# 128-row products in an attention prologue and tail, padded key buffers, and another order of maxima, masks, units and PV

## The chip, the cores and the metric

The kernel runs on one core of one Trainium2 chip. The metric is the device time in microseconds of one execution. Five engines work side by side, each through its own list of instructions, and wait for each other by semaphores: TensorE (PE, its weight loads are PEld), VectorE (DVE), ScalarE (ACT), GpSimd (POOL) and SyncE (SP, which issues most transfers).

## The reference

A macaron layer over 2 x 1024 tokens of width 128: half a feed-forward network, attention, half a feed-forward network again, each with a layer norm in front and a residual around it.

```python
    x = L0_attn_hidden_states
    x = x + 0.5 * _L0_ffn_ref(_layernorm(x, axis=-1), ...)
    x = x + _L0_attn_ref(_layernorm(x, axis=-1), ...)
    x = x + 0.5 * _L0_ffn_ref(_layernorm(x, axis=-1), ...)
```

The network `_L0_ffn_ref` is a mixture of experts: one shared expert of 352 hidden channels and the best 2 of 7 routed ones. The attention has 16 heads of 8 channels and works causally; its keys are the normalised tokens themselves:

```python
        v = x @ w_v + v_b
        q = (x @ w_q + q_b) @ w_k.T + k_b
        kh = x.reshape(b, s, H, D).transpose(0, 2, 1, 3)
        scores = jnp.einsum('bhqd,bhkd->bhqk', qh, kh) * scale
        scores = jnp.where(causal[None, None], scores, mask_value)
        probs = jax.nn.softmax(scores, axis=-1)
        out = jnp.einsum('bhqk,bhkd->bhqd', probs, v)
        out = out @ c_proj_w + c_proj_b
```

## The kernel before

Three stages follow one another: the first network (`ffn_*` with f = 0), the attention (`attn_*`), the second network (f = 1).

The attention takes the 2 batches x 16 heads as 8 groups of four heads. Queries and keys of a group stand in SBUF as 128 rows: head j of the four has the rows 32j to 32j + 31 (`head_rows(j)`), in which high and low parts of its 8 channels stand, and two rows for the maximum. There are three buffers of each, `K.keys[v]` and `K.queries[v]`, used in turn. A score product takes only its head's 32 rows, so it fills a quarter of the rows of TensorE's array. Rows of the profile name it `32*128`.

A group is worked on twice. First come the **maxima**: 40 products of queries by keys (`m_unit_pe`, L1609), ten kinds (`MAX_ORDER`) by four heads, each into one bank of PSUM. DVE reduces each to its maximum (`ring_dve`, L1785). Sixteen of the 40 are unmasked and 512 keys wide. The other 24 touch the diagonal: ahead of the product, `mask_pe` (L1599) writes the mask into the bank with four small products of 32 columns, one per column group. Four banks (`RING`) are used in turn, so PE is at most four maxima ahead of DVE. After the last maximum DVE negates and splits them (L1789 to L1793), PE transposes them (`mrow`), and SP moves them into two rows of each head's queries (`rows_load`).

Then come the **units**: 40 products of keys by queries with the maximum already in them (`unit_pe`, L1652), in three banks in turn. ACT takes the exponential of each (L1841). GpSimd zeroes what lies above the diagonal (`mask_pool`, L1890), and twelve **PV** steps (`pv_pe`, L1693) multiply probabilities by values, four heads in the four column groups at once, on all 128 rows. Results go through ACT (`ot`), a transpose on PE (`out`) and a division on DVE.

The order of this work is written by hand. The prologue (`attn_pe`) runs the 40 maxima of group 0 and the first `LEAD` maxima of group 1; between them stand steps for the second batch (`SECOND_PE`, `SECOND_DVE`): layer norm (z, its transposes L590), the q products (L1498 to L1500) and the v products. From `UNITS_FROM` on, a unit of group 0 stands ahead of each maximum. Then eight bodies follow, one per group (`pe_body`): six of the kind LOOP, one LAST_BUT_ONE and one LAST. In a body run the rest of the next group's maxima, the first `LEAD` of the one after, the units from number 12 on and the next group's first 12, and the PV steps. `ORDERS` says with a letter each in which order PE takes them: K a mask, R the next of the ring (maximum, mrow or out), U a unit, a a PV step, E a step of what comes after the attention. `OUT_AT` and `MT_LATER` place the out and mrow steps among the maxima, and `OEV_BEHIND` ACT's copies of the output among its exponentials. LAST_BUT_ONE has maxima only in its first part, LAST has none; I call what follows the last maximum the tail.

SP loads keys and queries of the group after the next in each body (`stack_load`, `keys_load`). GpSimd scatters the rows of the networks (`scatter_pool`, L1214, and L1191), each followed in part of the list by a small memset as a pause (`pause_pool`, L1201).

Of the kernel before, what the change touches and what calls it, by code (L numbers as in the profile page):

```python
# [29 lines left out]
P = 128  # L30
# [116 lines left out]
MAX_ORDER = (1, 2, 0, 3, 6, 7, 8, 4, 5, 9)  # L147
# [64 lines left out]
LEAD = 22  # L212
MT_LATER = 3
OUT_AT = (10, 24)
# [23 lines left out]
ORDERS = ['KKRUURKaKKURRUURaKKKURRURUaaKKRURURKKRURUaKKUURRKKURURKKUURRRURaRUUURRRRURRUaRURRUUaURRUaUURRaRURURUKaKURRUKKRRUUKKaURRU', 'KKRUURKaKKURRUURaKKKURRURUaaKKRURURKKRURUaKKUURRKKURURKKUURRUaUUURRRUUaUEUUaUEUaUUaUUEUaUUUEUaUU', 'RUUaUUEUaUUEUEaaUUUUEaUUUUUUUEaUUURUUaUUUaUaaEaaW']  # L238
# [49 lines left out]
def place_memory(K, ctx):  # L288
# [65 lines left out]
    with ExitStack() as s:  # L354
        zt = [sb(f"zt_{part}", [P, TOKENS], F32R, scope=s) for part in ("h", "l")]
        with ExitStack() as s2:
# [106 lines left out]
    K.ranked = sem("ranked")  # L463
# [948 lines left out]
def pad_pool(K, f):  # L1412
# [3 lines left out]
    K.nc.gpsimd.memset(K.act[:, :, HID:], 0.0).then_inc(K.padded0, 1)  # L1416

# [186 lines left out]
def m_unit_pe(K, n, r_bank, u):  # L1604
# [11 lines left out]
def ring_pe(K, what, d, n, p, u, r, r_bank):  # L1616

    e, v = K.nc.tensor, (u + d) % 3
    if r >= len(RING) and not (what == "max" and masked(n)):
        e.wait_ge(K.A["taken"], r + 1 - len(RING))  # L1620
# [4 lines left out]
    if what == "max":  # L1625
        if n == 0:
            e.wait_ge(K.ld_k[v], 32 * loads(p, u, d))
        ins = m_unit_pe(K, n, r_bank, v)
# [11 lines left out]
def unit_pe(K, p, u, d, n, start=False):  # L1640
# [3 lines left out]
    v, at0 = (u + d) % 3, 0  # L1644
# [54 lines left out]
def pe_body(K, p, u, kind):  # L1699
# [4 lines left out]
    for what in ORDERS[kind]:  # L1704
        if what == "U":
# [687 lines left out]
```

## Time and profile before

| | |
|---|---|
| median of 3 runs | 572.92 us (568.94 to 573.08) |
| the profiled execution | 574.49 us, span 572.7 us |
| PE busy | 527.5 us, 92% of the span |
| PE weight loads | 374.0 us, 65% |
| DVE busy | 386.9 us, 68% |
| ACT busy | 320.7 us, 56% |
| POOL busy | 269.8 us, 47% |

The span is cut into 40 slices of 14.3 us here. A digit is the busy share in tenths; PEclk is the clock that TensorE was granted, in tenths of the full 2.4 GHz, so a 5 is 1.2 GHz:

```profile
PE   5988879989999999999999999999899989899995
DVE  4696635557396397989999999973453775445744
ACT  4553434448343247787777878777555434434643
PEclk9899989999955558999999999979758999899998
```

The attention lies between about 157 and 437 us, slices 11 to 30. The groups that cost most of it, with the mean of one in ns and the idle time of the engine ahead of them:

```profile
L1785 DVE TENSOR_REDUCE mxp<-psum 128x1 f32<-128x512 f32 (+3 forms) x320 | 181.0, 630 | 32.3 <-PE psum L1609 32.2
L1841 ACT ACTIVATE probs<-psum 128x512 f32<-128x512 f32 x256 | 136.7, 600 | 45.1 <-PE psum L1652 44.1
L1609 PE MATMUL psum<-keys,queries 32*128 32x512 f32 (+3 forms) x384 | 107.7, 465 | 1.2 <-DVE mxp L1785 1.0
```

### The profile page before, as it was taken

What the parts mean: (1) busy time and instruction counts of PE and PEld (TensorE: products, weight loads), DVE (VectorE), ACT (ScalarE), POOL (GpSimd) and SP (SyncE); (2) the same over time, 40 slices, a digit from 0 to 9 for tenths busy, and PEclk for the clock granted to TensorE, in tenths of its full rate; (3) what the DMA queues carried; (4) which work ended last, traced back from release to release, by engine and by line L of the source; (5) the groups of instructions that cost most, each with busy time, mean ns of one, the idle gap of its engine ahead of it and who ended that gap; (6) DMA issues with size and microseconds to landing.
All of it is one profiled execution on the core that took longest, in us unless ns stands there. A gap on an engine that the chain in (4) does not pass through costs nothing.

```text
span 572.7 us, 12932 instructions
## 1 busy us (share of the span) xinstructions
PE 527.5 (92%) x4358; PEld 374.0 (65%) x4358; DVE 386.9 (68%) x1029; ACT 320.7 (56%) x694; POOL 269.8 (47%) x417
## 2 busy tenths in 40 slices
PE   5988879989999999999999999999899989899995
PEld 2888879988845654453444444345445889899994
DVE  4696635557396397989999999973453775445744
ACT  4553434448343247787777878777555434434643
POOL 8299887656583310304131111111308888854440
PEclk9899989999955558999999999979758999899998
DMA  8921424132761250405142231200001031431414
GB/s 280 291 70 48 113 75 126 43 103 85 229 181 46 74 186 2 175 2 174 28 149 79 99 137 39 102 2 2 2 0 34 30 90 43 123 90 41 130 39 116
DMA packets 40814, 52.65 MB, mean 92 GB/s; under 512 B 5616, under 2 KB 31728, under 8 KB 40112
## 3 DMA queue, kind: packets, MB, share of 16 engines
q1 hardware_dynamic: 31088, 39.03, 22.5%
q0 software_dynamic: 4480, 9.25, 4.9%
q10 hardware_dynamic: 5184, 3.55, 2.1%
q8 instruction: 38, 0.62, 0.5%
q14 instruction: 24, 0.20, 0.1%
HBM read 31.93 MB, written 28.00 MB: 105 GB/s over the span
## 4 chain that ended last, share of the span: by engine, by line
PE 51%; DVE 25%; issue 12%; DMA 5%; SPq 4%; POOL 2%; ACT 1%; DVEq 0%; ACTq 0%; POOLq 0%
DVE mxp L1785 19%; PE psum L1609 8%; PE psum L950 7%; PE psum L1693 6%; PE psum L1652 5%; PE psum L936 4%; PE psum L918 4%; PE psum L1599 3%; PE psum L916 3%; PE psum L917 3%; SPq L1275 2%; DMA wall_f<-in_ffn_sd 1%; DMA yc<-y_rows 1%; PE psum L1636 1%; POOL z_rows L1191 1%
## 5 line engine op out<-in xcount | busy, mean ns | idle before, releaser
L1785 DVE TENSOR_REDUCE mxp<-psum 128x1 f32<-128x512 f32 (+3 forms) x320 | 181.0, 630 | 32.3 <-PE psum L1609 32.2
L1841 ACT ACTIVATE probs<-psum 128x512 f32<-128x512 f32 x256 | 136.7, 600 | 45.1 <-PE psum L1652 44.1
L1609 PE MATMUL psum<-keys,queries 32*128 32x512 f32 (+3 forms) x384 | 107.7, 465 | 1.2 <-DVE mxp L1785 1.0
L1017 ACT ACTIVATE silu<-psum 128x352 f32<-128x352 f32 x107 | 49.6, 463 | 95.5 <-PE psum L918 70.2
L1652 PE MATMUL psum<-queries,keys 32*128 32x512 f32 (+3 forms) x384 | 99.7, 446 | 1.8 <-ACT probs L1841 1.8
L1214 POOL DMA_INDIRECT y_rows<-ys,to_row x76 | 74.2, 977 | 56.7 <-DVE ys L1096 30.7
L1060 DVE TENSOR_TENSOR act<-silu,psum 128x352 f32<-128x352 f32 x107 | 55.5, 519 | 65.1 <-ACT silu L1017 35.1
L950 PE MATMUL psum<-wall_f,at 128*128 (+1 forms) x648 | 92.1, 279 | 2.4 <-DVE x L1098 1.7
L1890 POOL TENSOR_SCALAR_AFFINE_SELECT probs<-probs 128x512 f32<-128x512 f32 x48 | 29.5, 635 | 131.6 <-ACT probs L1841 131.6
L950 PEld LDWEIGHTS psum<-wall_f,at 128*128 128x128 f32 x648 | 82.0, 194 | 3.8 <-issue 2.6
L1693 PE MATMUL psum<-probs,vg 128*32 128x512 f32 (+2 forms) x640 | 76.8, 555 | 0.0
L1652 PEld LDWEIGHTS psum<-queries,keys 32*128 32x128 f32 x384 | 50.6, 196 | 40.1 <-ACT probs L1841 18.7
L1609 PEld LDWEIGHTS psum<-keys,queries 32*128 32x128 f32 x384 | 50.4, 203 | 32.7 <-DVE mxp L1785 24.8
L936 PE MATMUL psum<-ident,act 128*128 128x128 f32 x324 | 54.6, 278 | 7.5 <-DVE act L1060 6.7
L916 PE MATMUL psum<-wall,zs_h 128*128 x152 | 56.5, 372 | 1.7 <-DVE zs_l L1084 1.7
L1025 ACT COPY at<-psum 128x384 f32<-128x384 f32 x108 | 51.3, 475 | 11.4 <-PE psum L936 8.1
L1599 PEld LDWEIGHTS psum<-ident_b,mask_b 128*32 128x32 bf16 x768 | 20.6, 97 | 47.1 <-DVE mxp L1785 27.8
L1599 PE MATMUL psum<-ident_b,mask_b 128*32 128x128 bf16 (+1 forms) x768 | 46.0, 261 | 5.1 <-DVE mxp L1785 3.6
L917 PE MATMUL psum<-wall,zs_h 128*128 x152 | 50.2, 330 | 0.0
L918 PE MATMUL psum<-wall,zs_l 128*128 x152 | 50.0, 329 | 0.0
L936 PEld LDWEIGHTS psum<-ident,act 128*128 128x128 f32 x324 | 41.0, 142 | 13.4 <-DVE act L1060 10.2
L1191 POOL DMA_INDIRECT z_rows<-zrow,slots x32 | 34.8, 1086 | 16.1 <-DVE slots L767 10.8
(245 smaller groups left out, 798.3 us busy)
## 6 DMA issues: line engine op xcount, KB each, us to landing
z_rows<-q_stack SPq DMA_DIRECT2D x12, 682.5 KB, 5.8
keys<-k_stack SPq DMA_DIRECT2D x8, 512.0 KB, 6.3
queries<-q_stack SPq DMA_DIRECT2D x8, 512.0 KB, 5.1
zg_early<-z_rows SPq DMA_DIRECT2D x44, 65.0 KB
yc<-y_rows SPq DMA_DIRECT2D x10, 256.0 KB, 4.2
zg_late<-z_rows SPq DMA_DIRECT2D x32, 65.0 KB
yc<-y_rows ACTq DMA_DIRECT2D x6, 256.0 KB, 4.1
wall_f<-in_ffn_rd SPq DMA_DIRECT2D x1, 1344.0 KB, 16.8
```

What stands on the lines that cost most here:

```text
L916: e.matmul(dst, zh, weight(K.wall, base, hi, HID), start=True, stop=False)
L917: e.matmul(dst, zh, weight(K.wall, base, lo, HID), start=False, stop=False)
L918: ins = e.matmul(dst, zl, weight(K.wall, base, hi, HID), start=False, stop=True)
L936: ins = e.transpose(bank(K, at_bank(f, q))[:, k * P:(k + 1) * P], K.act[:, q % 2, k * P:(k + 1) * P], K.ident[:, :])
L950: ins = e.matmul(bank(K, Y_BANK)[:, 0:EMB], K.at[:, q % 2, k * P:(k + 1) * P], weight(K.wall_f, base, DN + k * EMB, EMB), start=(k == 0), ...
L1214: e.indirect_dma_start(K.y_dram[f], bass.IndirectOffsetOnAxis(ap=K.to_row[:, j:j + 1], axis=0), K.ys[:, j % RING_Y, :], None).then_inc(K.y ...
L1599: e.matmul(dst[:, :, (nb - 1) * P:], K.mask_b[:, head_rows(c)], K.ident_b[:, :].unsqueeze(1).to_broadcast([P, len(parts), P]), start=True, ...
L1609: ins = K.nc.tensor.matmul(bank(K, r_bank)[:, start:start + nb * P], K.queries[u][head_rows(j), i * P:(i + 1) * P], K.keys[u][head_rows(j) ...
L1652: ins = e.matmul(slot(K, u, d, n)[:, at0:at0 + q1 - q0], K.keys[v][head_rows(j), kt * P:(kt + 1) * P], K.queries[v][head_rows(j), q0:q1], ...
L1693: ins = e.matmul(bank(K, O_BANK)[32 * j:32 * j + 32, q0 - half * CHUNK:q1 - half * CHUNK], K.vg[:, kt, j, :], probs_of(K, n)[:, j, :], sta ...
L1785: e.tensor_reduce(dst, scores, AX.X, ALU.max).then_inc(K.A["taken"], 1)
L1841: e.activation(strip_of(K, w)[:, j, :], slot(K, u, d, n)[:, 0:strip_width(w)], ACT.Exp, scale=SCALE).then_inc(K.A["ex"], 1)
```

## The change

It has four parts.

1. The key buffers become four times as large: `K.keys[v]` is [128, 4, 1024], and head j's keys stand in its 32 rows of slice j. `keys_load` loads them with four transfers in place of one. For the buffers 0 and 1 GpSimd fills the whole with zeros before (`wipe_pool`, 16 memsets, in place of the pauses behind the scatters 10 to 25 of the first network), and SP waits for these before the first load of keys. `probs_narrow` moves to another place in SBUF.
2. With them a product can take all 128 rows: the other heads' rows meet zeros. `m_whole_pe` does so for a maximum, with one mask product of 128 columns behind the product instead of four of 32 ahead of it; `unit_pe` with `whole` does so for a unit. All maxima and units of the prologue are of this kind, and the units behind the last maximum: the letters u in the orders of LAST_BUT_ONE and LAST. The loop's products stay at 32 rows.
3. `LEAD` is 20, not 22: the prologue has 62 steps of the ring and not 64, and LAST_BUT_ONE two maxima more.
4. `MAX_ORDER`, `OUT_AT`, `MT_LATER`, `OEV_BEHIND` and the three `ORDERS` are others.

```diff
-MAX_ORDER = (1, 2, 0, 3, 6, 7, 8, 4, 5, 9)
+MAX_ORDER = (0, 1, 3, 2, 6, 7, 4, 8, 5, 9)
-LEAD = 22
-MT_LATER = 3
-OUT_AT = (10, 24)
+LEAD = 20
+MT_LATER = 2
+OUT_AT = (0, 24)
...
-        if j < (WHOLE if f else WHOLE + 16):
+        if j < WHOLE:
             pause_pool(K)
+        elif f == 0 and j < WHOLE + 2 * WIPES:
+            wipe_pool(K, *divmod(j - WHOLE, WIPES))
...
+def wipe_pool(K, u, part):
+
+    e, n = K.nc.gpsimd, SEQ // 2
+    if (u, part) == (0, 0):
+        e.wait_ge(K.w_lo, len(WEIGHTS))
+        e.wait_ge(K.sw_lo, 5)
+        e.wait_ge(K.ld["const"], 16 * N_CONST_DMA)
+    j, half = divmod(part, 2)
+    e.memset(K.keys[u][:, j, half * n:(half + 1) * n].bitcast(F32), 0.0).then_inc(K.wiped, 1)
...
-                                 K.keys[u][head_rows(j), k0 * P:(k0 + nb) * P], start=not masked(n), stop=True,
+                                 K.keys[u][head_rows(j), j, k0 * P:(k0 + nb) * P], start=not masked(n), stop=True,
...
+def m_whole_pe(K, n, r_bank, u):
+
+
+    e, (parts, j) = K.nc.tensor, MAXES[n]
+    nb = parts[0][2]
+    dst = bank(K, r_bank)[:, 0:len(parts) * nb * P].rearrange("p (a k) -> p a k", k=nb * P)
+    for a, (i, k0, _) in enumerate(parts):
+        ins = e.matmul(dst[:, a, :], K.queries[u][:, i * P:(i + 1) * P], K.keys[u][:, j, k0 * P:(k0 + nb) * P],
+                       start=True, stop=True, skip_group_check=True)
+    if masked(n):
+        ins = e.matmul(dst[:, :, (nb - 1) * P:], K.mask_b[:, :],
+                       K.ident_b[:, :].unsqueeze(1).to_broadcast([P, len(parts), P]), start=False, stop=True,
+                       skip_group_check=True)
+    return ins
...
-    v, at0 = (u + d) % 3, 0
+    v, at0, rows = (u + d) % 3, 0, slice(0, P) if whole else head_rows(j)
...
-        ins = e.matmul(slot(K, u, d, n)[:, at0:at0 + q1 - q0], K.keys[v][head_rows(j), kt * P:(kt + 1) * P],
-                       K.queries[v][head_rows(j), q0:q1], start=True, stop=True, skip_group_check=True)
+        ins = e.matmul(slot(K, u, d, n)[:, at0:at0 + q1 - q0], K.keys[v][rows, j, kt * P:(kt + 1) * P],
+                       K.queries[v][rows, q0:q1], start=True, stop=True, skip_group_check=True)
...
-    K.nc.sync.dma_start(K.keys[v][:, :].bitcast(F32), K.k_dram[at(row, 4)].rearrange("g r t -> (g r) t"))\
-     .then_inc(K.ld_k[v], 16)
+    for j in range(4):
+        K.nc.sync.dma_start(K.keys[v][32 * j:32 * j + 32, j, :].bitcast(F32),
+                            K.k_dram[at(row + j, 1)].rearrange("g r t -> (g r) t")).then_inc(K.ld_k[v], 16)
...
-    e.wait_ge(K.w_lo, len(WEIGHTS))
-    e.wait_ge(K.sw_lo, 5)
+    e.wait_ge(K.wiped, 2 * WIPES)
     keys_load(K, 0, 0, 0)
```

What this makes of TensorE's list shows at three places. A row is a line, the operation, its output, its two operands and its size, and xN says that N like it follow one another. Lines are those of each kernel: products of maxima are L1609 before and L1637 (128 rows) or L1623 (32 rows) now, masks L1599 and L1640 or L1613, units L1652 and L1682, PV L1693 and L1723, out transposes L1636 and L1666.

TensorE in the prologue, from the first group's sixteen unmasked maxima on. Before:

```order
L1609 MATMUL psum<-keys,queries 128x512 x16
L1599 MATMUL psum<-ident_b,mask_b 32x128 x4
L1609 MATMUL psum<-keys,queries 128x384
L1599 MATMUL psum<-ident_b,mask_b 32x128 x4
L1609 MATMUL psum<-keys,queries 128x384
```

Now:

```order
L1637 MATMUL psum<-keys,queries 128x512 x16
L1637 MATMUL psum<-keys,queries 128x384
L1640 MATMUL psum<-ident_b,mask_b 128x128
L1637 MATMUL psum<-keys,queries 128x384
L1640 MATMUL psum<-ident_b,mask_b 128x128
```

The four small masks ahead of a product have become one behind it.

TensorE where the first loop body meets its first PV of 512 columns. Before:

```order
L1609 MATMUL psum<-keys,queries 128x384
L1652 MATMUL psum<-queries,keys 128x512 x2
L1609 MATMUL psum<-keys,queries 128x384
L1599 MATMUL psum<-ident_b,mask_b 32x2x128 x4
L1693 MATMUL psum<-probs,vg 32x512 x4
L1599 MATMUL psum<-ident_b,mask_b 32x2x128 x8
```

Now:

```order
L1682 MATMUL psum<-queries,keys 128x512 x2
L1666 MATMUL psum<-ident,ot 128x128 x4
L1613 MATMUL psum<-ident_b,mask_b 32x128 x12
L1623 MATMUL psum<-keys,queries 128x384 x3
L1723 MATMUL psum<-probs,vg 32x512 x4
L1613 MATMUL psum<-ident_b,mask_b 32x128 x8
L1682 MATMUL psum<-queries,keys 128x512
L1623 MATMUL psum<-keys,queries 128x384
```

The out transposes have come to the head of the body, and three masks and three products in one piece ahead of the PV.

TensorE in the last body, at the step that feeds the slots of the second network (`r_sel`). Before:

```order
L1652 MATMUL psum<-queries,keys 128x512 x7
L730 MATMUL psum<-r_sel,before_b 128x128
L731 MATMUL psum<-r_sel,ones_b 128x128
L1693 MATMUL psum<-probs,vg 32x512 x4
L1652 MATMUL psum<-queries,keys 128x512
```

Now:

```order
L1682 MATMUL psum<-queries,keys 128x512 x2
L1723 MATMUL psum<-probs,vg 32x512 x4
L1682 MATMUL psum<-queries,keys 128x512 x4
L1723 MATMUL psum<-probs,vg 32x512 x4
L1682 MATMUL psum<-queries,keys 128x512
L728 MATMUL psum<-r_sel,before_b 128x128
L729 MATMUL psum<-r_sel,ones_b 128x128
```

Seven units in a row are split by PVs, and the slots' step stands behind two more PVs than before.

## Rows read from the trace of the kernel before

**Rows 1.** The windows view: the stages between the two feed-forward networks

```profile
157.50:199.40 41.90, 40.60 (x184) 22.89 (x183) 26.66 (x59) 15.28 (x35) 21.07 (x35) 0.53 0.34 103
199.40:218.30 18.90, 17.74 (x104) 9.07 (x104) 15.07 (x29) 7.37 (x15) 2.89 (x5) 0.52 0.44 142
244.50:270.60 26.10, 24.95 (x301) 11.81 (x298) 24.32 (x49) 20.42 (x43) 6.48 (x10) 1.00 0.28 97
349.10:377.60 28.50, 27.37 (x301) 12.47 (x298) 24.34 (x49) 20.52 (x43) 5.23 (x9) 0.89 0.16 52
388.30:402.00 13.70, 13.70 (x109) 8.08 (x105) 4.49 (x16) 9.88 (x21) 2.49 (x4) 1.00 0.01 4
402.00:408.80 6.80, 5.76 (x28) 2.03 (x27) 3.83 (x13) 2.62 (x6) 4.73 (x9) 0.50 0.00 0
415.60:432.70 17.10, 16.10 (x63) 6.67 (x67) 8.88 (x42) 9.10 (x20) 3.66 (x5) 0.50 0.03 9
```

**Rows 2.** The windows view: two microseconds around the clock's fall and its rise

```profile
158.00:160.00 2.00, 1.10 (x3) 0.40 (x3) 1.97 (x4) 0.00 (x0) 1.02 (x1) 0.91 0.26 76
216.00:218.00 2.00, 2.00 (x21) 0.56 (x16) 0.34 (x1) 0.59 (x2) 0.00 (x0) 0.58 0.05 12
```

**Rows 3.** The chain of waits in the prologue: start, duration, what

```profile
157.00 0.11 PE psum L1499
...
166.14 0.23 PE psum L1599 x3
166.37 0.61 PE psum L1609
...
187.80 0.43 PE psum L1499
...
190.01 0.21 PE psum L1499
```

**Rows 4.** The timeline of the prologue: start, duration, engine, line, operation, [idle before]

```profile
171.88 1.65 ACT L557 ACTIVATE z<-x,mr_neg,rstd 128x128 f32<-128x128 f32 x4 [5.17 <-POOL mr_neg L538]
...
175.48 1.65 ACT L557 ACTIVATE z<-x,mr_neg,rstd 128x128 f32<-128x128 f32 x4
...
173.84 1.11 PE L590 MATMUL psum<-ident,z 128*128 128x128 f32 x4
...
179.94 1.11 PE L590 MATMUL psum<-ident,z 128*128 128x128 f32 x4
...
187.00 0.80 PE L1498 MATMUL psum<-zt_h,wq_h 128*128 128x512 f32 x1
...
199.39 0.22 DVE L1789 TENSOR_REDUCE nmax<-mxp 128x32 f32<-128x64 f32 x1
```

**Rows 5.** The timeline of VectorE in one loop body

```profile
257.97 9.73 DVE L1785 TENSOR_REDUCE mxp<-psum 128x1 f32<-128x512 f32 x17
267.91 1.95 DVE L1785 TENSOR_REDUCE mxp<-psum 128x1 f32<-128x384 f32 x4 [0.21 <-PE psum L1609]
270.63 1.89 DVE L1785 TENSOR_REDUCE mxp<-psum 128x2 f32<-128x512 f32 x3 [0.78 <-PE psum L1609]
```

**Rows 6.** The chain of waits in the loop and in the tail

```profile
268.99 0.92 PE psum L1693 x8
...
419.04 1.87 PE psum L1693 x8
...
422.31 2.26 PE psum L1652 x4
...
437.35 0.59 ACT ot L1854
```

**Rows 7.** The timeline of GpSimd: a scatter, a memset, a late scatter

```profile
108.81 0.97 POOL L1214 DMA_INDIRECT y_rows<-ys,to_row  x1 [0.58 <-DVE ys L1096]
...
182.07 0.95 POOL L1931 MEMSET ot<- 128x1024 f32 x1
...
435.07 0.97 POOL L1191 DMA_INDIRECT z_rows<-zrow_late,slots  x1 [0.16 <-issue]
```

More of the change, by code:

```diff
@@ L462, in place_memory @@
     K.padded, K.blank, K.padded0 = sem("padded"), sem("blank"), sem("act_padded")
-    K.ranked = sem("ranked")
+    K.wiped, K.ranked = sem("wiped"), sem("ranked")
     K.NS = [{n: sem(f"n{k}_{n}") for n in
@@ L1613, in m_unit_pe, with ring_pe @@
     return ins
-def ring_pe(K, what, d, n, p, u, r, r_bank):
+def m_whole_pe(K, n, r_bank, u):
[10 more added lines that the diff above has]
+    return ins
+def ring_pe(K, what, d, n, p, u, r, r_bank, whole=False):
     e, v = K.nc.tensor, (u + d) % 3
-    if r >= len(RING) and not (what == "max" and masked(n)):
+    if r >= len(RING) and (whole or not (what == "max" and masked(n))):
         e.wait_ge(K.A["taken"], r + 1 - len(RING))
@@ L1626, in ring_pe @@
         if n == 0:
-            e.wait_ge(K.ld_k[v], 32 * loads(p, u, d))
-        ins = m_unit_pe(K, n, r_bank, v)
+            e.wait_ge(K.ld_k[v], 80 * loads(p, u, d))
+        ins = (m_whole_pe if whole else m_unit_pe)(K, n, r_bank, v)
     elif what == "mrow":
@@ L1637, in ring_pe, with unit_pe @@
     ins.then_inc(K.A["ring"], 1)
-def unit_pe(K, p, u, d, n, start=False):
+def unit_pe(K, p, u, d, n, start=False, whole=False):
     e = K.nc.tensor
     w, j = UNITS[n]
-    v, at0 = (u + d) % 3, 0
+    v, at0, rows = (u + d) % 3, 0, slice(0, P) if whole else head_rows(j)
     if not start:
@@ L1704, in pe_body @@
     for what in ORDERS[kind]:
-        if what == "U":
-            unit_pe(K, p, u, *units.pop(0))
+        if what in "Uu":
+            unit_pe(K, p, u, *units.pop(0), whole=what == "u")
         elif what == "R":
@@ L1759, in attn_pe @@
         if r >= UNITS_FROM:
-            unit_pe(K, 0, 0, 0, r - UNITS_FROM, start=r - UNITS_FROM < 3)
-        if what == "max" and masked(n):
-            mask_pe(K, n, r, RING[r % len(RING)])
-        ring_pe(K, what, d, n, 0, 0, r, RING[r % len(RING)])
+            unit_pe(K, 0, 0, 0, r - UNITS_FROM, start=r - UNITS_FROM < 3, whole=True)
+        ring_pe(K, what, d, n, 0, 0, r, RING[r % len(RING)], whole=True)
     for n in range(len(RING_PROLOGUE) - UNITS_FROM, AHEAD):
-        unit_pe(K, 0, 0, 0, n, start=n < 3)
+        unit_pe(K, 0, 0, 0, n, start=n < 3, whole=True)
     for p in range(LOOP3):
@@ L1964, in keys_load, with rows_load @@
     v, row = (u + d) % 3, count(p, u, 4, 4 * d)
-    K.nc.sync.dma_start(K.keys[v][:, :].bitcast(F32), K.k_dram[at(row, 4)].rearrange("g r t -> (g r) t"))\
-     .then_inc(K.ld_k[v], 16)
-def rows_load(K, p, u, d, r):
+    for j in range(4):
+        K.nc.sync.dma_start(K.keys[v][32 * j:32 * j + 32, j, :].bitcast(F32),
+                            K.k_dram[at(row + j, 1)].rearrange("g r t -> (g r) t")).then_inc(K.ld_k[v], 16)
+def rows_load(K, p, u, d, numbers):
     e, v = K.nc.sync, (u + d) % 3
-    e.wait_ge(K.ld_k[v], 32 * loads(p, u, d))
+    e.wait_ge(K.ld_k[v], 80 * loads(p, u, d))
     alone(K, e)
     for part in range(2):
-        e.wait_ge(K.A["taken"], r + part + 1)
+        e.wait_ge(K.A["taken"], numbers[part] + 1)
         dst = K.queries[v][part:part + 97:32, :].bitcast(F32).rearrange("j (i q) -> j i q", q=P)
@@ L1984, in sp_body @@
         stack_load(K, p, u, 2)
-    rows_load(K, p, u, 1, count(p, u, RINGN, RING0[kind] + RINGS[kind].index(("mrow", 1, 0))))
+    rows_load(K, p, u, 1, [count(p, u, RINGN, RING0[kind] + RINGS[kind].index(("mrow", 1, n))) for n in range(2)])
     if kind == LOOP:
@@ L2011, in attn_sp @@
     queries_load(K, 0, 0, 1)
-    rows_load(K, 0, 0, 0, RING_PROLOGUE.index(("mrow", 0, 0)))
+    rows_load(K, 0, 0, 0, [RING_PROLOGUE.index(("mrow", 0, n)) for n in range(2)])
     for c in range(NCH // 2, NCH):
```

15 lines of the change are left out of this document (7 added, 8 removed).

## Prediction

> **What bounds the kernel now.** I first read the page: the span is 572.7 us, TensorE is busy 92% of it, and the clock line has a run of fives in slices 13 to 16, between the two feed-forward networks. I then cut the attention into stages with the windows view [rows 1]; its columns are the stretch, its length, the busy time of PE, PEld, DVE, ACT and POOL, the granted clock, the DMA share and GB/s. Three regimes stand there.
>
> In the prologue (157.5 to 218.3) PE is busy 40.60 of 41.90 us and then 17.74 of 18.90, at 0.53 and 0.52 of the clock, so at 1.2 GHz, while DVE, which reads every maximum, is busy 26.66 and 15.07. TensorE is the bound, and it is slow.
>
> In the loop (one body is 26.1 us, there are six) the clock is 1.00 and DVE is busy 24.32 of 26.10: DVE is the bound, with about 1.8 us of gaps. One body of the series fell to 0.89 and took 28.50, 2.4 more [rows 1].
>
> In the tail, behind the last maximum (388.3 to 437.2), DVE has little to do; PE is busy 13.70 of 13.70 at full clock, and 5.76 of 6.80 and 16.10 of 17.10 in two stretches at half clock. ACT is busy 9.10 of the last 17.10. TensorE is the bound again.
>
> Why is the clock low? In the windows of 2 us it falls in the stretch where the 32-row products of the maxima take over from 128-row products (0.91 in 158 to 160, then 0.50), and rises in the one in which the first PV of 512 columns, which uses all 128 rows, has just run (0.58 in 216 to 218, then 1.00) [rows 2]. Between the two PE was never idle for long. So what goes with the low clock is not waiting, but the kind of product: 32 rows of 128. The page "TensorE: Matmul & The Clock Gate" of the Trainium skill (Part 1) says that a monitor sets the clock by how busy PE has been recently; read as busy time alone, the trace disagrees here, with a full row of busy PE at half clock. By that reading padding would not help; that is the first rival below.
>
> **The prologue, part by part.** The change makes each product 128 rows by zeros around a head's keys, and replaces four masks of 32 columns with one of 128.
>
> Masked maxima: now 0.23 for the masks and 0.61 for the product [rows 3], 0.84 in all. Nothing in the trace is exactly the new pair. A 512-column, 128-row product steps in 0.43 at half clock, and a 128-column one in 0.21 at half and 0.11 at full clock [rows 3]. A 384-column product and its mask are then 0.32 + 0.21 = 0.53 at half, and about 0.27 at full. DVE needs 1.95 for four, 0.49 each [rows 5]. So the pair costs DVE's pace at either clock, almost. An unmasked maximum is paced by DVE at 9.73 / 17 = 0.57 (a little low, since the group's end overlaps; I use 0.6) [rows 5], and 0.43 or 0.21 on PE is hidden behind it.
>
> But DVE's pace is not the whole path; the second half of the tokens is normalised in between. I follow the landmarks [rows 4]:
> The first z ends at 171.88 + 1.65 = 173.5, and its transposes start at 173.84. They do not depend on the maxima's clock, so nothing is gained up to there. The second z ends at 175.48 + 1.65 = 177.1, but its transposes start at 179.94, behind five masked maxima. With those at 0.5 to 0.6 they start at 177.1 to 177.5: 2.6 gained. Transposes and the q product last from 179.94 to 182.3 and are halved: 1.1. Five more maxima bring the second q at 187.00, 4.7 later; PE may run four slots ahead of DVE, so 5 x 0.6 = 3.0 is the most and 1.7 is possible: 1.7 to 3.0 gained. From 187.00 to the last maximum at 199.39 are q (0.43 x 3), 24 v products at 0.21 and five masked maxima: q and v at full clock give 0.65 + 24 x 0.10 = 3.0, the five masked ones about 0.35 each, 1.7; some of DVE's 3 us waits there go with them. Sum 2.6 + 1.1 + 2.3 + 4.7 = 10.7, and with run-ahead up to 13. I take 11.
>
> From 199.39 to the loop's first two-part maximum at 218.3 are 18.9 us. DVE's work is 16 x 0.6 + 8 x 0.49 + 1.4 for the negated maxima and their rows = 14.9. The regular loop loses 0.78 in front of that maximum [rows 5], so 3.2 of the 4.0 are the half clock's. I take 3. The units that stand beside maxima here ran in other row groups at the same time; 128-row ones follow one another. At full clock that is 0.21 + 0.21 against DVE's 0.6, and hidden. Prologue: **-14**, bounds -8 (the clock comes only part of the time) and -16.
>
> **What it adds.** Sixteen memsets of 128 x 512 stand where 16 pauses of the scatter stream stood. A memset of 128 x 1024 takes 0.95, so one of these 0.48 by halves, and GpSimd waits there for DVE (0.58) in any case [rows 7]. SP now waits for all sixteen before it loads the first keys; the last stands behind the 26th scatter of 38, well ahead of the first maximum. Zero; if the load came late, it would be at most its 6.3 us (the page's section 6). Each keys load is four transfers of a quarter: three more issues of about 0.4 on SP, behind which stand the rows of the maxima, but they wait for DVE 20 us later. Zero. Two lead maxima go from prologue to the last body but one: 2 x 0.49 less and more on the same engine. Zero.
>
> **The loop's order.** The instructions are the same; only their order changes, with 31 changes between column-tiled and row-tiled work before and 30 now. In a body DVE waits 0.78 behind PV0 (0.92 on PE) and 0.21 a few times [rows 5, 6]. Now PV0 stands behind three finished products of 0.49, which covers 1.47 of PE work, so most of the 0.78 goes. But the out transposes and three masks now stand at the body's start, and PV1 and PV2 follow one another with only two maxima in front: 0.5 to 0.8 comes back. I take 0 per body, with -0.8 and +0.8 as bounds: 0, from -5 to +5 for six. One body in six may still fall to the low clock, as now.
>
> The page "TensorEngine Tiling (Array Packing)" (Key Properties) says that a change of tiling mode drains TensorE. Padding takes such changes away in the prologue; the trace does not separate this from the clock, and the sum has no term for it.
>
> **The tail.** 415.6 to 432.7 has 16.10 us of PE at half clock: 8.05 at full. One PV of 512 falls from 1.87 to 0.92, and six of a group's twelve PVs are that wide [rows 6]. The 17 units in it lose their overlap: four took 2.26 with waits at half clock [rows 6]; at full a 128-row unit needs 0.21, and in pairs about half of it was free, so 0.15 each, 2.5 more. That is 10.6, about ACT's 9.10 plus its first wait: 11 against 17.1, 6 gained. 402 to 408.8: 5.76 halved, plus 0.8, plus about 1.3 of waits for ACT and GpSimd: 5 against 6.8, 2 gained. 388.3 to 402 already had the full clock and a full PE, so the lost overlap costs there: 17 units at 0.15 would be 2.5; where ACT's exponentials pace the units, which is 9.88 of the 13.70 [rows 1], it costs nothing; +1. In the last body the step that gives GpSimd its slots now stands behind two more PVs (2 x 0.92); the stream of scatters that matters starts at 435.07, behind the last mask, and not with the slots, so zero. Tail: **-7**, bounds -10 and -1. The gain reaches the end: the ot copy at 437.35 and GpSimd's scatters from 435.07 on wait for it [rows 6, 7], and from there the rows go through GpSimd without a gap to the second network.
>
> **Sum.** -14 + 0 - 7 = -21. The profiled execution took 574.5 (span 572.7 and 1.8 around it), which is 1.6 above the median of 572.92. 574.5 - 21 = 553.5, in terms of the median **552**.
>
> **Rivals.**
> The clock stays low (5% for the same, 3% for slower). What speaks for it is busy PE at half clock [rows 2]; against it, that 128-row work ran at full clock on either side. Masks and pairs still gain: about 0.3 x 20 in the prologue less what is hidden, -5; units beside maxima then need 0.43 + 0.43 against 0.6, 12 x 0.26 = +3; the tail's some 22 units in half-clock stretches lose 0.25 each, +5.5, and +1: +4.5, so 577. If the padded units also lose the clock where it was full (13.7 + 6.8 us double, less ACT's share), it is +15 to +20: 592. It decides once the gain of the prologue is under 7 and the tail is at half clock throughout. The page "TensorE: Matmul & The Clock Gate" (Part 3) speaks for this side: it has 32-row products in different row groups run concurrently, 3.07 times as fast for four; the trace agrees that unit and maximum start together.
>
> Half of it (15%): the clock returns in one of the two places. In the prologue alone, -14 and +1: 560; in the tail and late in the prologue, -8 and -7 or less: 558 to 562.
>
> The order costs (5%): the heads of the bodies, with the out transposes and seven masks between PV11 and PV0, lose 0.8 or fall to the low clock more than once, 2.4 each: +5 to +8: 559.
>
> The forecast itself has 72%, its own range 546 to 557.
>
> **The numbers.** A measurement tells a change of about 1% (5.7 us) from none. Under 567.2: 0.72 + 0.15 + 0.05 = 0.92; within 1%: 0.05; above 578.6: 0.03. 545 to 563 leaves out the low clock's 0.08 and some 0.1 at both edges.
>
> **What would show it.** Right: a clock near 1.00 from about 177 on in the prologue, at the latest behind the second transposes; masked pairs at 0.5 to 0.6; the last maximum of the first group near 188 and not 199; a body of 26.1; the tail at 1.00 with PE busy through, the ot copy at about 416. Wrong: 0.50 with padded products running; DVE waits in a body above 2.5 us; the first maximum later than 158, which would be the memsets.

## The result and the profile after

The changed kernel takes 551.41 us (median of 4 runs, 548.75 to 555.12) against 571.51 for the kernel before on the same chip: 0.966 of it, 95% interval 0.958 to 0.973. The forecast was 552, faster. The profiled execution took 553.19 us, its span is 551.4.

The page after. PE, DVE and ACT are busy shares by slice of 13.8 us, PEclk is the granted clock; then two groups of part 5:

```profile
PE   6897879998988899999999999999898989899995
...
DVE  5686644547568899998999898985654775445744
ACT  4563434448544477776777776788673434344643
...
PEclk9899998999995899998999998999999999899999
```

```profile
L1813 DVE TENSOR_REDUCE mxp<-psum 128x1 f32<-128x512 f32 (+3 forms) x320 | 180.0, 628 | 20.6 <-PE psum L1623 13.7
...
L1623 PE MATMUL psum<-keys,queries 32*128 32x512 f32 (+3 forms) x316 | 71.5, 417 | 1.1 <-DVE o_all L1834 1.1
```

Of the five fives in the clock line before, one is left, and DVE's idle time ahead of its maxima fell from 32.3 to 20.6 us. The windows view of the attention after, columns as in [rows 1]: prologue up to the last maximum of group 0, from there to the loop, two loop bodies, and the tail in three pieces:

```profile
157.00:186.80 29.80, 25.92 (x112) 16.80 (x110) 25.71 (x59) 14.01 (x34) 19.17 (x31) 0.77 0.49 144
186.80:208.77 21.97, 20.62 (x183) 12.32 (x183) 20.53 (x39) 13.63 (x25) 4.76 (x10) 0.92 0.45 123
263.72:290.51 26.79, 26.22 (x301) 12.73 (x298) 24.59 (x49) 20.08 (x42) 6.48 (x10) 1.00 0.30 95
317.30:345.49 28.19, 27.64 (x301) 13.03 (x298) 24.59 (x49) 20.08 (x42) 5.23 (x9) 0.94 0.30 89
376.40:390.00 13.60, 13.60 (x109) 9.05 (x105) 4.96 (x19) 10.17 (x22) 2.49 (x4) 1.00 0.02 4
390.00:404.00 14.00, 12.51 (x97) 6.73 (x93) 7.64 (x25) 9.84 (x20) 5.54 (x10) 1.00 0.01 2
404.00:420.00 16.00, 13.79 (x100) 7.11 (x93) 8.30 (x41) 10.24 (x21) 8.19 (x12) 1.00 0.05 17
```

The prologue's stretch of 42.40 us (157.00 to 199.40) takes 29.80 now, with DVE's work nearly the same (25.71 busy; before 26.66). The tail is at 1.00 throughout. But a loop body without a fall of the clock takes 26.79, where it took 26.10 in [rows 1].

Four landmarks cut every profile of this study: DVE's first maximum, the last maximum of group 0 (the first `nmax`), that of group 7 (the last `nmax`), and the last `ot` copy. After:

```profile
157.32 10.58 DVE L1813 TENSOR_REDUCE mxp<-psum 128x1 f32<-128x512 f32 x18 [2.47 <-PE psum L1637]
...
186.80 0.22 DVE L1817 TENSOR_REDUCE nmax<-mxp 128x32 f32<-128x64 f32 x1
...
376.43 0.22 DVE L1817 TENSOR_REDUCE nmax<-mxp 128x32 f32<-128x64 f32 x1
```

```profile
417.67 0.58 ACT L1882 COPY ot<-psum 128x512 f32<-128x512 f32 x1 [0.35 <-PE psum L1723]
```

The differences of such rows, in us, with those of the experiments below. "Falls" are bodies of the loop in which the clock fell, in that one profiled execution. The last two columns are the median of the kernel before in the same session on the same chip, and the ratio to it with its 95% interval. Medians and ratios leave out executions in a slower state of the chip, as the profiled one of order_only was (586.77 us against 577.3 to 580.2 of its others), so its tail, 53.71 where the same list takes 48.20 in tail32, is compared with nothing below.

| kernel | first group | loop (falls) | tail | to the end | median | before, beside it | ratio |
|---|---|---|---|---|---|---|---|
| before | 41.36 | 188.40 (1) | 49.56 | 135.35 | 571.5 | | |
| after | 29.48 | 189.63 (2) | 41.24 | 133.73 | 551.4 | 571.5 | 0.966 (0.958 to 0.973) |
| after_again | 29.84 | 189.58 (2) | 41.25 | 132.21 | 552.5 | 570.2 | 0.972 (0.965 to 0.979) |
| order_only | 41.38 | 193.32 (1) | 53.71 | 136.94 | 579.0 | 573.4 | 1.009 (0.999 to 1.019) |
| products_only | 29.70 | 187.37 (2) | 44.37 | 135.51 | 550.9 | 573.4 | 0.962 (0.952 to 0.973) |
| prol32 | 41.36 | 190.31 (1) | 41.28 | 136.04 | 568.5 | 573.4 | 0.991 (0.983 to 0.998) |
| tail32 | 29.44 | 186.87 (0) | 48.20 | 136.07 | 564.0 | 573.4 | 0.984 (0.973 to 0.995) |
| small_masks | 34.52 | 188.29 (1) | 41.21 | 133.32 | 555.6 | 570.2 | 0.973 (0.966 to 0.981) |
| whole_mask | 40.23 | 193.23 (2) | 41.22 | 136.56 | 567.7 | 574.5 | 0.989 (0.980 to 0.998) |
| combo | 28.71 | 189.69 (3) | 41.59 | 132.27 | 550.8 | 570.2 | 0.966 (0.961 to 0.971) |
| combo_pv | 29.49 | 182.85 (0) | 41.60 | 133.83 | 546.0 | 570.2 | 0.957 (0.951 to 0.963) |
| combo_pv_again | 28.89 | 182.85 (0) | 41.59 | 136.62 | 549.0 | 575.7 | 0.955 (0.951 to 0.960) |
| filler | 29.91 | 182.87 (0) | 41.59 | 135.00 | 549.6 | 575.7 | 0.955 (0.950 to 0.960) |
| loop_mask | 29.93 | 294.46 (every body) | 43.93 | 136.16 | 668.1 | 574.5 | 1.166 (1.158 to 1.175) |

The way to the end moves by nearly 5 us and the first maximum by 3 us (156.5 to 159.6) among kernels that are equal there. These stages are read as noise. In between, the first group repeats within 1.2 us where nothing was changed, the loop within 0.1 us where prologue, order and number of falls are the same, and the tail of 128-row units within 0.1 us (41.2 in five rows, 41.6 in four).

### The profile page after: what moved, and what is told of

Read it like the earlier page. It is cut to its first block, busy times and chain, and to the rows that moved or that the text cites. A ratio compares the mean times of both kernels' runs of the same rounds, so it can differ in the third digit from the quotient of the medians.

```text
span 551.4 us, 12788 instructions
## 1 busy us (share of the span) xinstructions
PE 507.4 (92%) x4274; PEld 371.8 (67%) x4274; DVE 387.5 (70%) x1029; ACT 317.5 (58%) x694; POOL 271.3 (49%) x417
## 4 chain that ended last, share of the span: by engine, by line
PE 54%; POOL 16%; DVE 14%; issue 7%; DMA 6%; ACT 1%; ACTq 1%; SPq 0%; DVEq 0%; POOLq 0%
POOL z_rows L1189 10%; PE psum L1723 10%; DVE mxp L1813 9%; PE psum L1623 7%; PE psum L948 7%; PE psum L1682 6%; PE psum L934 3%; POOL idle L1199 3%; PE psum L1613 3%; PE psum L914 3%; PE psum L915 3%; PE psum L916 3%; DMA b_p<-in_attn_c_proj_b 2%; DMA yc<-y_rows 1%; PE psum L968 1%
## 5 line engine op out<-in xcount | busy, mean ns | idle before, releaser
L1813 DVE TENSOR_REDUCE mxp<-psum 128x1 f32<-128x512 f32 (+3 forms) x320 | 180.0, 628 | 20.6 <-PE psum L1623 13.7
L1682 PE MATMUL psum<-queries,keys 32*128 32x512 f32 (+7 forms) x384 | 96.2, 404 | 0.2 <-ACT probs L1869 0.2
L1723 PE MATMUL psum<-probs,vg 128*32 128x512 f32 (+2 forms) x640 | 71.1, 526 | 1.7 <-POOL probs L1918 1.7
L1623 PE MATMUL psum<-keys,queries 32*128 32x512 f32 (+3 forms) x316 | 71.5, 417 | 1.1 <-DVE o_all L1834 1.1
L1682 PEld LDWEIGHTS psum<-queries,keys 32*128 32x128 f32 (+1 forms) x384 | 51.0, 183 | 22.1 <-ACT probs L1869 14.6
L1623 PEld LDWEIGHTS psum<-keys,queries 32*128 32x128 f32 x316 | 33.4, 184 | 30.9 <-DVE mxp L1813 23.0
L1189 POOL DMA_INDIRECT z_rows<-zrow,slots x32 | 34.4, 1074 | 15.8 <-DVE slots L765 10.4
L1613 PEld LDWEIGHTS psum<-ident_b,mask_b 128*32 128x32 bf16 x656 | 16.3, 96 | 33.4 <-DVE mxp L1813 25.2
L1613 PE MATMUL psum<-ident_b,mask_b 128*32 128x128 bf16 (+1 forms) x656 | 33.3, 246 | 1.8 <-DVE mxp L1813 1.5
```

Source lines behind the costliest of these rows:

```text
L1189: e.indirect_dma_start(K.z_dram[f], bass.IndirectOffsetOnAxis(ap=K.slots[:, g:g + 1], axis=0), K.zrow[f][:, t, :], None).then_inc(K.z_sc[t ...
L1723: ins = e.matmul(bank(K, O_BANK)[32 * j:32 * j + 32, q0 - half * CHUNK:q1 - half * CHUNK], K.vg[:, kt, j, :], probs_of(K, n)[:, j, :], sta ...
L1813: e.tensor_reduce(dst, scores, AX.X, ALU.max).then_inc(K.A["taken"], 1)
```

## The experiments

### Order and products, apart

`order_only` is the changed kernel with every product on 32 rows again, `products_only` has the 128-row products in the order of before:

```diff
 # order_only: after, with
-        ring_pe(K, what, d, n, 0, 0, r, RING[r % len(RING)], whole=True)
+        if what == "max" and masked(n):
+            mask_pe(K, n, r, RING[r % len(RING)])
+        ring_pe(K, what, d, n, 0, 0, r, RING[r % len(RING)], whole=False)
 # whole=False at both calls of unit_pe in attn_pe too, and every u in ORDERS is U
 # products_only: after, with MAX_ORDER, LEAD, MT_LATER, OUT_AT, ORDERS,
 # OEV_BEHIND of before, and U -> u behind the last R of LAST_BUT_ONE and in LAST
```

> The changed order, LEAD 20 and the padded key buffers, but every product on 32 rows as before, the masks too. Theory (the order costs about 0.65 us a body, read from bodies of 26.8 against 26.15 us): 571.5 + 4 = 575.5 us, bodies of 26.8, clock near 0.5 in the prologue and in the tail as before. Rival (the order costs nothing and the longer bodies come from the lower clock in two of them): 571.5 us, bodies of 26.15. Rival (the wipes or the four transfers cost): the first maximum later than 158.0.

> The products on 128 rows in the prologue and behind the last maximum, with the padded buffers, in the order of before: MAX_ORDER, LEAD 22, MT_LATER, OUT_AT, ORDERS and OEV_BEHIND are those of before. Theory: 551.4 - 4 = 547 us, bodies of 26.15 with a clock of 1.00, the last maximum of the first group near 187. Rival (the order was chosen so that 128-row products gain, and without it the gain in the tail is smaller because units stand there in long rows): 553 to 556 us. Rival (order is neutral): 551 us.

One body of each without a fall, then one of products_only with one, in the windows view. order_only:

```profile
225.67:252.46 26.79, 26.25 (x301) 12.72 (x298) 24.59 (x50) 20.08 (x42) 5.25 (x9) 1.00 0.30 95
```

products_only:

```profile
229.47:255.63 26.16, 25.02 (x301) 11.83 (x298) 24.33 (x49) 20.45 (x43) 6.48 (x10) 1.00 0.31 97
255.63:284.08 28.45, 27.30 (x301) 12.39 (x298) 24.34 (x49) 20.56 (x43) 6.48 (x10) 0.89 0.29 89
```

The body goes with the order alone: 26.79 with the new one on 32 rows everywhere, 26.16 with the old one. So the order costs 0.64 us a body. In exchange most falls of the clock cost less in it: 1.4 (28.19 against 26.79) in place of 2.3 to 2.4, in all eight falls of after, after_again, prol32, small_masks and whole_mask; order_only's own fall, left out for the reason given with the table, cost 3.7. With the new order alone the kernel is not faster than before (interval 0.999 to 1.019), 5.6 us above it by the medians where the theory had 4.

products_only lands at 550.9, the number of the rival "order is neutral", and not at 547. In its profiled execution the loop is only 2.3 shorter than after's, because the clock fell twice at 2.3, and the tail is 3.1 longer. The second is what the other rival said: with the units in long rows the clock fell in the tail although they have 128 rows, in a stretch in which TensorE stood idle for about half the time (busy 1.07 of 2 us, 400 to 402):

```profile
401.00:408.00 7.00, 6.61 (x23) 3.65 (x22) 3.63 (x15) 3.50 (x8) 0.00 (x0) 0.51 0.01 2
```

That execution took 556.66, the other three 550.1 to 551.5 at a higher mean clock, so the two falls cannot be carried over to the median.

Where the 0.64 arises, in the timeline of VectorE after:

```profile
263.72 3.15 DVE L1813 TENSOR_REDUCE mxp<-psum 128x1 f32<-128x512 f32 x6 [0.85 <-PE psum L1623]
...
279.80 1.95 DVE L1813 TENSOR_REDUCE mxp<-psum 128x1 f32<-128x384 f32 x4 [0.42 <-PE psum L1623]
...
286.59 3.08 DVE L1813 TENSOR_REDUCE mxp<-psum 128x1 f32<-128x512 f32 x5 [0.21 <-PE psum L1623]
...
290.51 1.89 DVE L1813 TENSOR_REDUCE mxp<-psum 128x1 f32<-128x512 f32 x3 [0.84 <-PE psum L1623]
```

PV0 stands behind three finished products now, and I read the 0.42 in front of 279.80 as what is left there. But the old 0.78 came back as 0.85 at the wide PV behind the twelve small masks at 289.88. DVE's idle time in a body is 2.20, before 1.78 (26.79 - 24.59 and 26.10 - 24.32); the other 0.27 is longer busy time of DVE, and which piece of the order causes it was not separated.

### Prologue and tail, apart

```diff
 # prol32: the prologue as in order_only, the tail as in after
 # tail32: the tail as in order_only, the prologue as in after
```

> The changed kernel with the 32-row products and small masks back in the prologue alone; the tail keeps 128 rows. Theory (the prologue's gain is that of the clock, 11.9 us up to the last maximum of the first group and 2.4 behind it): 551.4 + 14 = 565 us, clock near 0.5 from 160 to 217. Rival (half of the gain in the prologue is the order's): 558 us.

> The changed kernel with the 32-row units back in LAST_BUT_ONE and LAST alone; the prologue keeps 128 rows. Theory (8.3 us from the last maximum to the last ot copy come from the products): 551.4 + 8 = 559.5 us, clock 0.5 in two stretches behind the last maximum. Rival (the new place of the PVs among the units gives them): 552 us, the clock at 1.00 without the 128-row units.

prol32 has the first group at 41.36, exactly that of before. Its loop without its fall is 188.9 (190.31 - 1.4), that of after without its two 186.8 (189.63 - 2.8), so the prologue is worth 11.9 + 2.1 = 14.0 by the traces. The medians, 568.5 and 551.4, stand 17 apart, more than the 14 expected, but they come from two sessions; the ratios to the kernel before, 0.991 and 0.966, differ by 0.025, which is 14.3 us. tail32 has a tail of 48.20 against 41.24, so the 128-row units are worth 7.0 of the 8.3 in this execution, and the clock went low as before. At 564.0 it missed the theory (559.5), and the rival (552) by far. The profiled execution was the fastest of its four, and the ratio of 0.984 against 0.966 makes the units worth 10.4 us (with intervals that still touch), so 7.0 is rather a lower end. The windows view of tail32:

```profile
387.00:398.00 11.00, 9.69 (x45) 5.16 (x44) 6.41 (x25) 4.95 (x12) 5.54 (x10) 0.53 0.00 0
407.00:422.00 15.00, 14.06 (x60) 5.23 (x61) 6.47 (x36) 7.86 (x16) 6.47 (x9) 0.54 0.04 13
```

The rival, that the new place of the PVs alone gives the tail's gain, falls: with the new places and 32-row units both stretches are at half clock. But the places do matter beside 128-row units: with the old ones (products_only) the tail takes 44.37 and the clock falls once, with the new ones 41.24 and it does not. Padding alone is worth 5.2 (49.56 against 44.37), and the other 3.1 want both.

### Clock or masks: what the prologue gains from

The change does two things to a masked maximum at once: its product takes 128 rows, and its mask is one product instead of four. `small_masks` undoes only the second (its masks stay behind the product), `whole_mask` only the first (and puts the prologue's units back on 32 rows):

```diff
 # small_masks, in m_whole_pe
-    ins = e.matmul(dst[:, :, (nb - 1) * P:], K.mask_b[:, :], ...)
+    for c in range(4):
+        ins = e.matmul(dst[head_rows(c), :, (nb - 1) * P:], K.mask_b[:, head_rows(c)], ...)
 # whole_mask, in m_whole_pe
-        ins = e.matmul(dst[:, a, :], K.queries[u][:, ...], K.keys[u][:, j, ...], ...)
+        ins = e.matmul(dst[:, a, :], K.queries[u][head_rows(j), ...], K.keys[u][head_rows(j), j, ...], ...)
```

> The changed kernel with four masks of 32 columns behind each 128-row product in the prologue, in place of one of 128. Theory (the gain is the clock's, given by the 128-row products): the same clock in the prologue, four small masks take 0.13 to 0.25 us at full clock and stay under DVE's 0.49 with their product; the last maximum of the first group at most 2 us later, 552 to 554 us. Rival (most of the gain is that of fewer masks and fewer changes of tiling): the last maximum 5 us or more later, 557 us or more.

> The changed kernel with the products of maxima and the units of the prologue back on 32 rows, but the mask still one of 128 columns behind the product. Four small masks behind a 128-row product cost 5.0 us up to the last maximum of the first group (34.5 us from the first maximum in that kernel, 29.5 in the changed one, 41.4 before). Theory (the clock is given by 128-row products, the mask's form is a cost of its own): clock near 0.5 until the first wide PV at about 215, from the first to the last maximum of the group 36 to 38 us (41.4 less 3.5 to 5), 560 to 563 us in all. Rival (the four small masks alone kept the clock low): the clock back by 180, 30 us, 553 us.

A 384-column pair at half clock is the time from one product's start to the next. After, in the timeline of TensorE:

```profile
167.61 0.67 PE L1637 MATMUL psum<-keys,queries 128*128 128x384 f32 x1
168.08 0.33 PE L1640 MATMUL psum<-ident_b,mask_b 128*128 128x128 bf16 x1
168.17 0.67 PE L1637 MATMUL psum<-keys,queries 128*128 128x384 f32 x1
```

small_masks:

```profile
168.62 0.69 PE L1637 MATMUL psum<-keys,queries 128*128 128x384 f32 x1
169.24 0.30 PE L1641 MATMUL psum<-ident_b,mask_b 128*32 128x128 bf16 x4
169.46 0.69 PE L1637 MATMUL psum<-keys,queries 128*128 128x384 f32 x1
```

whole_mask:

```profile
168.54 0.69 PE L1637 MATMUL psum<-keys,queries 32*128 32x384 f32 x1
169.16 0.29 PE L1640 MATMUL psum<-ident_b,mask_b 128*128 128x128 bf16 x1
169.37 0.69 PE L1637 MATMUL psum<-keys,queries 32*128 32x384 f32 x1
```

The pairs take 0.56, 0.84 and 0.83; before it was 0.23 + 0.61 = 0.84 [rows 3]. Neither half of the change gives anything at a given clock; both together give 0.28. What the three dear pairs have in common is that product and mask cut the array in different ways (128*32 beside 128*128, 32*128 beside 128*128, and before 128*32 beside 32*128), whichever way round and however many masks; I read the 0.27 to 0.28 us as the price of a change there and back at half clock. "TensorEngine Tiling (Array Packing)" (Key Properties) of the Trainium skill says that changing the tiling mode drains TensorE; the trace agrees as far as each change there and back goes with this price, and does not show the drain itself.

The clock is the larger part. small_masks was at half clock from 164 to 185, not to 178, and then had the full one for the v products: its first group is 6.8 shorter than before (34.52 against 41.36) and 5.0 longer than after. My theory allowed it 2 us and 552 to 554 in all; it took 555.6. whole_mask stayed at half clock from 160 to 215, nearly as before, and gained 1.1; the theory allowed 3.5 to 5 (560 to 563 us, it took 567.7), and that missed on the same ground, a mask in one piece not being cheaper beside a 32-row product. So the 11.9 us are 6.8 for the clock with 128-row products, and 5.0 more once the masks are of the same tiling, part of it a clock that comes back 7 us sooner.

`filler` puts unneeded 128-row work into the prologue of the fastest kernel (below), to see whether the clock follows it:

```diff
+        if whole and r < 26:
+            filler_pe(K, bank(K, r_bank), 4 if r < 16 else 2)
         ins = (m_whole_pe if whole else m_unit_pe)(K, n, r_bank, v)
```

> The same kernel with work added: ahead of each of the first 26 products of the prologue one 128-row product of constants (512 columns for the sixteen unmasked, 256 for the next ten) into the same bank, which the product then overwrites. In the changed kernel TensorE waits there for DVE, is busy 0.73 to 1.8 of 2 us, and the clock falls at 164 and stays at 0.50 to 177.7. Theory (the clock is kept by the 128-row work that TensorE does): clock at 1.00 from 164 to 178 in spite of, and because of, the added work, pairs of 0.36 + 0.11 us, the last maximum of the first group 28 to 29.5 us behind the first maximum in place of 29.5, 544.5 to 546 us. Rival (the clock falls where maxima run, whatever the rows): half clock, each masked pair 0.21 longer, the last maximum 2 us later, 548 us.

Its windows of 2 us (columns as above):

```profile
163.00:165.00 2.00, 2.00 (x9) 0.76 (x8) 2.00 (x5) 1.58 (x6) 2.00 (x6) 1.00 0.63 169
165.00:167.00 2.00, 2.00 (x8) 0.68 (x7) 2.00 (x4) 2.00 (x8) 1.86 (x4) 1.00 0.12 29
...
173.00:175.00 2.00, 0.25 (x3) 0.10 (x2) 1.97 (x10) 1.65 (x4) 1.23 (x4) 0.72 0.50 197
175.00:177.00 2.00, 2.00 (x10) 1.84 (x10) 0.70 (x3) 0.94 (x3) 0.62 (x2) 0.50 0.00 0
```

After, with the one ahead of the fall as well:

```profile
161.00:163.00 2.00, 1.65 (x4) 0.71 (x4) 2.00 (x4) 1.60 (x6) 2.00 (x6) 1.00 0.71 194
163.00:165.00 2.00, 1.80 (x4) 0.78 (x4) 2.00 (x4) 2.00 (x8) 1.86 (x4) 0.77 0.11 27
165.00:167.00 2.00, 2.00 (x7) 1.17 (x6) 2.00 (x5) 1.19 (x5) 2.00 (x2) 0.50 0.71 220
...
173.00:175.00 2.00, 2.00 (x9) 1.39 (x9) 1.03 (x3) 0.96 (x3) 0.60 (x2) 0.50 0.00 0
```

The clock stayed full until 173.9 and fell when TensorE stood waiting for z (0.25 us busy of 2). Counted from the first maximum that is 14.5 us; without the added work it was 5.8 to 7.1 (after, combo_pv and combo_pv_again). The filler raised TensorE's 128-row work and its busy time together, from 1.65 to 2.00 of 2 us; a filler of 32-row products, which would tell the two apart here, was not run. It gained no time: the first group took 29.91 against 28.89 and 29.49 of the kernel without it. DVE, busy all along, sets the pace there; that the low clock then came in a worse place is argued. 549.6 against 549.0 is no difference, and 544.5 to 546 was missed.

### The two orders put together

`combo` takes the loop's order, LEAD, MAX_ORDER and OUT_AT of before and the tail's order of after. `combo_pv` moves two PVs of its loop body (the expectation says three; the third letter stayed where it was):

```diff
 # combo: ORDERS[0] of before; ORDERS[1] of before up to RRR, then as below; ORDERS[2] of after
+ ...RRRauuuEauuuEauuuauuEuauuuEauuu
 # combo_pv, end of ORDERS[0] (R product, U unit, K masks, a PV)
-...RRUaUUURRaRURURUKaKURRUKKRRUUKKaURRU
+...RRUaUUURRRURUaRUKKURRUaKKRRUUKKaURRU
```

The changed kernel ran beside them:

> The changed kernel once more, beside the next runs on one chip: 551 us, bodies of 26.8 us, 28.2 where the clock falls in one.

> The 128-row products with the loop order, LEAD, MAX_ORDER and OUT_AT of before, and in the tail (behind the last maximum of LAST_BUT_ONE, and LAST) the order of the changed kernel. Theory (the changed order costs 0.65 us a body and gains 3.1 us in the tail, against the tail of products_only at 44.4 us): loop bodies of 26.15, 28.5 where the clock falls; 182.6 us from the last maximum of the first group to that of the last if it never falls and 187.4 if it falls twice, against 189.6; the tail at 41.2: 544 to 549 us. Rival (the tail gains only behind its own loop): 551 us with a tail of 44.

> The kernel above with three PVs of the loop body moved behind three, two and three more units or products, so that the stretch between the bunch of wide PVs and the next body's PV0, in which the low clock began in both falls of products_only (278 and 332 us), holds more 128-row work. Theory (the clock falls where a stretch is poor in 128-row products): no fall in the loop, bodies of 26.15, 2.4 us less for each fall that the kernel above has: 543 to 545 us. Rival (the falls come at random or from something else): as many falls, no gain. Rival (the later PVs hold ACT up): bodies longer than 26.3.

Medians of 6 runs: 552.5 (551.3 to 558.2) for the changed kernel, 550.8 (549.7 to 552.5) for combo, 546.0 (544.3 to 548.2) for combo_pv. In combo the clock fell in three bodies (at 224, 278 and 333 us), each time in the same place, ahead of the products in two parts, which then wait 2.41. So combo missed its 544 to 549, in which two falls had been reckoned with, and combo_pv its 543 to 545 by one. Combo's tail is 41.59, not 44 as the rival said, so the new tail's order does carry over: 2.8 of the 3.1.

combo_pv, a body in the windows view, and its first and last `nmax`:

```profile
228.46:254.62 26.16, 25.30 (x301) 12.09 (x298) 24.34 (x49) 20.44 (x43) 6.49 (x10) 1.00 0.31 97
```

```profile
186.62 0.22 DVE L1817 TENSOR_REDUCE nmax<-mxp 128x32 f32<-128x64 f32 x1
...
369.47 0.22 DVE L1817 TENSOR_REDUCE nmax<-mxp 128x32 f32<-128x64 f32 x1
```

No body fell, and the loop takes 182.85, 6.8 less than in after or combo. The ranges of the runs do not overlap with either. The number of falls has some chance in it, though: the changed order had two, one or none in the same loop (tail32 none), and products_only, with the loop of combo, two in the profiled execution and a higher mean clock in the other three. What stands against chance here is that three profiled executions with the moved PVs (this one and the two below) had none.

> The kernel with the order of before, three PVs moved, and 128-row products in prologue and tail, once more beside the next one: 546 us, no fall of the clock between 192 and 464 us, 182.9 us from the last maximum of the first group to that of the last.

It took 549.0 (548.5 to 550.6), 3 more than the first time, though the loop again took 182.85 without a fall. The profiled executions differ behind the `ot` copy (133.8 and 136.6), where nothing was changed, and the kernel before took 5.6 more beside it too. Its ratio to before was 0.957 and 0.955, against 0.966 and 0.972 of the changed kernel. It beats both kernels.

### One mask in the loop too

`loop_mask` is combo_pv with `mask_pe` left out of the bodies and one mask of 128 columns behind each masked 32-row product.

> The 546 us kernel (order of before with three PVs moved, 128-row products in prologue and tail) with the mask of every maximum in the loop bodies and LAST_BUT_ONE also one of 128 columns behind its product, the product still on 32 rows. In the prologue a pair with four small masks took 0.84 us at half clock and 0.59 at full, with one mask 0.56 and 0.36. Theory (a small mask costs its own start and a change of tiling, DVE is the bound of the loop and TensorE 1 us behind it): bodies of 25.5 to 26.1 in place of 26.15, 542 to 546 us. Rival (masks ahead of time fill TensorE's free moments, a mask behind the product lengthens DVE's waits, and units cannot run beside a 128-row mask): bodies of 26.5 or more, 548 us or more.

668.1 us, 1.166 of before (1.158 to 1.175). A body of it:

```profile
216.50:260.10 43.60, 43.60 (x229) 18.11 (x226) 26.05 (x50) 21.52 (x42) 5.23 (x9) 0.66 0.18 58
```

Neither theory came near. There are 72 matmuls fewer than in 301, TensorE is never idle, and yet the body is 17.4 longer, because the clock is at half for about 31 of 43.6 us, which is worth 15 to 16 of the 17.4 in an engine that is busy throughout: it falls with TensorE fully busy. This is the strongest case here that busy time alone doesn't hold the clock. "TensorE: Matmul & The Clock Gate" (Part 1) of the Trainium skill says that the clock is set by how busy TensorE has been recently; read as busy time alone, this trace disagrees. Each pair brings a 32-row product, two changes of tiling and a mask over the whole array, so the wide 128-row PVs come further apart; at half clock they come further apart still. That the low clock starts and so keeps itself is argued from the order of the list; what the runs show is the length and the clock of the bodies.

## Why the prediction was right, point by point

- **Prologue, -14.** Measured: 11.9 up to the first `nmax`. Behind it the old loop takes 188.40, and 182.85 + 2.4 for its one fall leave 3.15 for the half clock at its head. 15.0 in all; in the new order prol32 gives 14.0. The landmarks came as forecast: second transposes at 177.13 (177.1 to 177.5), second q at 181.07 (181.0 by the steps' sum), last maximum at 186.80 (188). The clock was back at 177.7.
- **What the forecast gave as its reason there** was only half right. It said that the change of tiling has no term in the sum. It had one without being named: the pair of 0.53 was put together from rows of one tiling, and only in one tiling it holds. 5.0 of the 11.9 hang on that, as small_masks shows.
- **The clock "near 1.00 from 177"** held, apart from 188 to 192 (combo_pv_again has no such dip, and the same loop of 182.85). What was not foreseen is that it held until 164 while unmasked maxima alone ran, and then fell though every product had 128 rows: TensorE waited for DVE (1.65 us busy of 2), and filler shows that more work of that kind keeps it, for nothing.
- **Wipes and key loads, 0.** First maximum at 157.32, before 158.03. Right, but not by that time: the forecast's sign, "later than 158", was met by order_only (159.55), prol32 (158.81), small_masks (158.16) and tail32 (158.92), which wipe and load in the same way. What settles it is that the first product of a maximum starts as soon as the last v product has gone (within 0.1 to 0.2 us in each of these kernels as before), so it waits for no load:

```profile
156.73 0.28 PE L1514 MATMUL psum<-wv_h,zt_l 128*128 128x128 f32 x1
156.84 9.09 PE L1637 MATMUL psum<-keys,queries 128*128 128x512 f32 x17
```

- **Order, 0 (bounds -5 to +5).** This is the term that was mis-sized. By order_only it is +0.64 a body, and +4.0 for the loop (tail32's 186.87 against combo_pv's 182.85, both without a fall), and two falls of 1.4 in place of one of 2.4 add 0.4. The step that failed is "0.5 to 0.8 comes back, so I take 0": 0.85 came back, but of the 0.78 that was to go, 0.42 stayed, and DVE's busy time grew by 0.27.
- **Tail, -7.** Measured -8.3. Padding alone gives 5.2 of it in the old order and 7.0 or more in the new one; that the new order adds 3.1 beside 128-row units was not in the forecast, which had nothing for the moved PVs but the slots' step. The clock was 1.00 throughout and the `ot` copy came at 417.67, 1.7 behind the forecast of 416, in a kernel whose loop had lost 4.4.
- **The sum.** -15.0 + 4.4 - 8.3 = -18.9, and 2.3 less in the front and at the end, which move by as much among equal kernels. That -21 was hit is partly luck: a missed +4.4 met a larger prologue and tail (2.3 together) and this other 2.3, which is noise.

The forecast's rival "half of it" is in kind what prol32 (568.5) and tail32 (564.0) show, both above its 558 to 562. "The order costs" (559) had the right mechanism and nearly the size (+4.4 against its +5 to +8), and was hidden by the larger gains.

## What to carry to other kernels

Look at TensorE's granted clock by stretch, and where it is low under full load, ask how many rows its products use: padding a 32-row product with zeros gave 6.8 us of a 41 us stage. Then keep neighbours in one tiling: at a given clock a pair got cheaper only with both halves of the change (0.84, 0.83, 0.84, and 0.56), and the mask in one piece beside 32-row products cost over 100 us in the loop. In a mixed loop try to spread the 128-row work evenly: two letters moved in an order table were worth 6.8 us of loop, where the whole new order had cost 4 there and gained 3 in the tail.

## What the runs showed of the hardware that was not expected

- A masked pair takes 0.27 to 0.28 us more at half clock if its two products cut the array differently, whichever of them is the small one.
- The clock can fall to 1.2 GHz and stay there with TensorE 100% busy (43.60 of 43.60 at 0.66), and with two PVs moved by a few instructions no body fell in three profiled executions, where the order of before had one to three falls in each of three.
- 128-row products do not keep the clock by themselves: in the prologue it fell at 164 us and in the tail of products_only at 401, both times with TensorE idle for part of the time just before (1.65 us busy of 2; 1.07 of 2).
- Work of no use kept the clock at 2.4 GHz for 7 to 9 us longer and cost nothing measurable, but it did not help, for the bound was elsewhere.
